# Last transformer of a four-layer kernel: scores of 128 queries in four quarters of the array, passes dealt to free slots, inverse norms by exp(-0.5 ln), a new plan of times

## The reference

```python
h = shift_token(x); q, k, v = split(h @ wqkv)        # 8 heads of 64
q, k = rotary_xpos(l2norm(q) * qs, l2norm(k) * ksc)  # l2norm: t / clip(norm(t), 1e-12)
# windows of 64 queries, each over its own and the previous 64 keys, causal within 64
attn = softmax(where(mask, -max, q @ k.T * 8)); o = attn @ v
x = x + o @ wo
h = layernorm(shift_token(x)) @ w1 + b1; a, g = split(h)   # 341 each
x = x + (a * gelu(g)) @ w2 + b2
```

## Time and profile before

| | |
|---|---|
| median of three runs | 3424.36 us |
| the profiled execution's own time | 3435.19 us |
| its span (first to last instruction) | 3433.9 us |
| mean granted TensorE clock | 0.884 of full |
| PE, DVE, ACT, POOL busy, share of the span | 83%, 70%, 56%, 47% |
| last stage, by the shift of its first pass and the end | 2491 us to 3434 us |
| table loads on ACT in the whole program | 222 of 1283 ns |

### The profile page before, as it was taken

How to read it: one execution, slowest core, us unless ns; L and a number is a source line. 1 busy time by engine, 2 the same in 40 slices (tenths; PEclk the granted TensorE clock), 3 DMA queues, 4 the chain that set the end, 5 groups by cost and what they waited for, 6 DMA issues and landing times.

```text
span 3433.9 us, 40196 instructions
## 1 busy us (share of the span) xinstructions
PE 2850.7 (83%) x14610; PEld 1219.9 (36%) x14610; DVE 2404.9 (70%) x2723; ACT 1939.1 (56%) x3566; POOL 1616.5 (47%) x989
## 2 busy tenths in 40 slices
PE   6799999966678888888876898888779898898876
PEld 3233333331223333333321532222245555555543
DVE  4888853369999999999895343877566666676562
ACT  2466662244577677677765413776545556656544
POOL 2212100224768887877876011555454445445341
PEclk6799999976788888888887998999889999999998
DMA  4132200021112221221313000111000000000000
GB/s 98 31 57 42 47 3 1 34 74 26 38 37 63 43 44 38 64 40 40 60 30 112 1 0 13 25 25 25 13 22 14 20 12 22 23 12 23 12 22 25
DMA packets 79729, 114.28 MB, mean 33 GB/s; under 512 B 16270, under 2 KB 49422, under 8 KB 78106
## 3 DMA queue, kind: packets, MB, share of 16 engines
q1 hardware_dynamic: 68268, 103.06, 12.8%
q0 software_dynamic: 11264, 8.66, 1.8%
HBM read 37.69 MB, written 17.33 MB: 16 GB/s over the span
## 4 chain that ended last, share of the span: by engine, by line
PE 43%; DVE 31%; ACT 12%; issue 8%; POOL 3%; DMA 1%; SPq 0%; DVEq 0%; POOLq 0%; ACTq 0%
DVE layer_mamba_state L1399 13%; DVE psum L1388 7%; ACT L142 3%; PE psum L830 3%; PE psum L2675 3%; PE psum L2706 2%; PE psum L2253 2%; PE psum L961 2%; PE psum L1249 2%; DVE layer_peak L771 2%; PE psum L2746 2%; ACT layer_p L2869 2%; PE psum L2689 2%; PE psum L1176 2%; PE psum L810 2%
## 5 line engine op out<-in xcount | busy, mean ns | idle before, releaser
L1441 POOL TENSOR_TENSOR layer_mamba_state<-layer_mamba_state,layer_mamba_c 128x1024 f32<-128x1024 f32 x320 | 783.0, 2482 | 287.7 <-DVE layer_mamba_state L1399 281.2
L1399 DVE TENSOR_TENSOR_SCAN layer_mamba_state<-layer_mamba_decay,psum 128x1024 f32<-128x1024 f32 x320 | 731.4, 2286 | 34.9 <-DVE psum L1388 1.0
L1249 PE MATMUL psum<-layer_mamba_state,two_to_one 128*64 128x512 f32 x1280 | 414.2, 735 | 53.8 <-DVE layer_mamba_x L1416 34.1
L771 DVE TENSOR_REDUCE layer_peak<-psum 128x2 f32<-128x1024 f32 x256 | 308.4, 1222 | 72.6 <-PE psum L742 68.0
L844 ACT ACTIVATE layer_exps<-psum 128x1024 f32<-128x1024 f32 x256 | 255.9, 1023 | 153.7 <-PE psum L810 153.7
L142 ACT ACT_TABLE_LOAD x222 | 284.8, 1283 | 66.3 <-DVE layer_scale L2969 22.9
L1328 ACT ACTIVATE layer_mamba_decay<-layer_mamba_delta_wide,layer_weights 128x511 f32<-128x511 f32 x384 | 250.4, 711 | 16.9 <-DMA layer_mamba_delta_wide<-layer_mamba_delta 8.9
L1388 DVE TENSOR_TENSOR psum<-psum,layer_mamba_u_wide 128x1024 f32<-128x1024 f32 x192 | 236.1, 1230 | 31.4 <-DMA layer_mamba_u_wide<-layer_mamba_work 20.6
L3063 POOL TENSOR_TENSOR layer_qk<-layer_qk,layer_v_between 128x1024 f32<-128x1024 f32 x64 | 150.7, 2354 | 207.3 <-DVE layer_v_between L2963 207.3
L3076 POOL TENSOR_TENSOR layer_p<-layer_p,layer_stats 128x512 f32<-128x512 f32 x128 | 132.7, 1040 | 240.0 <-DVE layer_stats L2999 239.9
L2869 ACT ACTIVATE layer_p<-psum,layer_stats 128x128 f32<-128x128 f32 x512 | 180.8, 369 | 89.3 <-DVE layer_stats L2992 86.6
(11 more groups left out here) (344 smaller groups left out, 5737.6 us busy)
## 6 DMA issues: line engine op xcount, KB each, us to landing
layer_mamba_delta_wide<-layer_mamba_delta SPq DMA_DIRECT2D x96, 128.0 KB, 2.3
layer_mamba_u_wide<-layer_mamba_work SPq DMA_DIRECT2D x96, 128.0 KB, 2.4
attn<-layer_mamba_delta SPq DMA_DIRECT2D x64, 128.0 KB, 2.4
attn<-layer_mamba_work SPq DMA_DIRECT2D x64, 128.0 KB, 2.4
layer_v_between<-layer_v SPq DMA_DIRECT2D x16, 512.0 KB, 4.3
qk_dram<-layer_qk_parts SPq DMA_DIRECT2D x16, 384.0 KB, 2.9
layer_q_rows<-qk_dram SPq DMA_DIRECT2D x96, 64.0 KB
layer_k_rows<-qk_dram SPq DMA_DIRECT2D x96, 64.0 KB
```

Source lines behind the costliest of these rows:

```text
L771: dve.tensor_reduce(self.peak[s][:, block, 2 * g:2 * g + 2], c.psum[:, at:at + 2, :], AX.X, ALU.max).then_inc(self.maxed, 1)
L1249: e = pe.matmul(c.psum[j * HALF:(j + 1) * HALF, self.sum_banks[h], :], c.two_to_one[:, :], self.state[i % len(self.state)][:, j, :], start ...
L1399: dve.tensor_tensor_scan(state, decay, self.fill.rearrange("p j t -> p (j t)"), 0.0, ALU.mult, ALU.add).then_inc(self.scanned, 1)
L1441: pool.tensor_tensor(state, state, self.both(self.c_wide[turn % self.C_BUFFERS][:, :]), ALU.mult).then_inc(self.multiplied, 1)
```

## The change

Four edits, all within `Ffn3` but for one mask.

1. Scores are taken for 128 queries, that is two windows, in one group: two mask products into two banks, then 16 score products. Head j of a pair writes bank j, window g of the block goes to array columns and PSUM partitions 64g to 64g+63, so that the four products (j, g) of a pair stand in four quarters of the array. The number of products is the same (72 for a pass). Maximum, exponentials, reciprocal, multiplication, transposes and copy are as many and as large as before, now by head j of the pair in place of window. The products with v of both windows stand in one group, which waits for both copies.
2. Passes are dealt out in the order (first four sequences, depth 0), (the same, depth 1), (last four, depth 0), (the same, depth 1), number n to slot n mod 3, a third of a period (127.5 planned us) apart: slot 0 has six passes, slots 1 and 2 have five.
3. The inverse norm is exp(-0.5 ln(max(squares, 1e-24))): a DVE maximum, then Ln and Exp on ACT, both in the table set that the exponentials use. Root and DVE reciprocal go.
4. The planned times of all steps are new.

```diff
+PLAN_F = FfnPlan(
+    make=(2.0, 9.8, 17.6, 25.4), ..., root=31.9, inverse=33.5, scale=(34.5, 32.21, 38.7, 40.38),
+    turn=(40.76, 44.24, 46.5, 48.22), ..., score=(42.38, 55.6, 68.6, 81.4), scored=(4.92, 5.52),
+    maxed=(2.0, 3.2), exp=(2.8, 5.0), sum_inverse=(5.14, 6.74), weight=(5.47, 7.7), weight_turn=(8.4, 9.96), ...
+    weight_kept=(9.2, 11.4), weigh=13.71, weighed=-0.17, keep=15.31, out=100.0, out_added=3.93,
+    ..., gelu=3.26, ..., mlp=125.8, mlp_added=3.48, gate=134.45, update=0.9, period=127.5)
+PASSES3 = [(half * SEQS // 2 + b, d) for half in range(2) for d in range(DEPTH) for b in range(SEQS // 2)]
...
-        for t, b in enumerate(range(s, SEQS, SLOTS3)):
-            for d in range(DEPTH):
-                r = t * DEPTH + d
-                yield b, d, r, (s / SLOTS3 + r) * PASS3
+        for n in range(s, len(PASSES3), SLOTS3):
+            yield *PASSES3[n], n // SLOTS3, n / SLOTS3 * PLAN_F.period
...
+    def pe_score(self, s, r, t, now):
...
+        banks = [self.banks.take(("scores", s, 2 * n + j), now, now + PLAN_F.scored[j]) for j in range(2)]
+        for at in banks:
+            c.wait_bank(at)
+            pe.matmul(c.psum[:, at, :], c.ident16[:, :], mask, start=True, stop=False)
         for i in range(PAIRS3):
-            for j in range(2):
-                rows = slice(DIM3 * j, DIM3 * (j + 1))
-                e = pe.matmul(c.psum[rows, at, i * P + gap:(i + 1) * P], q[rows, i, queries], k[rows, i, keys],
-                              start=False, stop=i == PAIRS3 - 1)
+            for j, g in ((0, 0), (1, 1), (0, 1), (1, 0)):
+                rows, window = slice(DIM3 * j, DIM3 * (j + 1)), 2 * t + g
...
+                e = pe.matmul(c.psum[g * WINDOW:(g + 1) * WINDOW, banks[j], i * P + gap:(i + 1) * P], q[rows, i, queries],
+                              k[rows, i, keys], start=False, stop=i == PAIRS3 - 1)
...
+    def pe_weigh(self, s, r, t, now):
+        own = self.banks.take(("heads_out", s, n), now, now + PLAN_F.weighed)
+        hold.wait_ge(self.p_kept[s], 2 * n + 2)
...
     def act_normalise(self, s, r):
-        self.c.table(SQRT_TABLE)
-        self.c.act.activation(scale[:, 1, :, :], scale[:, 0, :, :], ACT.Sqrt).then_inc(self.root[s], 1)
+        hold.wait_ge(self.squares_held[s], r + 1)
+        self.c.table(EXP_LN_TABLE)
+        act.activation(logs, squares, ACT.Ln).then_inc(self.root[s], 1)
...
+        act.activation(inverse, logs, ACT.Exp, scale=-0.5).then_inc(self.norms_made[s], 1)
...
     def dve_normalise(self, s, r):
-        dve.tensor_scalar(norms, norms, 1e-12, None, ALU.max).then_inc(made, 1)
-        dve.reciprocal(inverse, norms).then_inc(made, 1)
+        self.c.dve.tensor_scalar(squares, squares, 1e-24, None, ALU.max).then_inc(self.squares_held[s], 1)
```

More of the change, by code:

```diff
@@ L2323 @@
 HIDDEN_PACE3 = 1.2
[L2326 to L2335, removed]
@@ new lines @@
+PLAN_F = FfnPlan(
+    make=(2.0, 9.8, 17.6, 25.4), qkv=(0.0, 1.2, 2.4), made=(5.06, 3.5, 2.77), square=(1.2, 2.4), values=-0.1,
+    rotate=(2.28, 3.58), sums=6.53, add=4.7, root=31.9, inverse=33.5, scale=(34.5, 32.21, 38.7, 40.38),
+    turn=(40.76, 44.24, 46.5, 48.22), turned=(2.37, 2.22, 2.9), score=(42.38, 55.6, 68.6, 81.4), scored=(4.92, 5.52),
+    maxed=(2.0, 3.2), exp=(2.8, 5.0), sum_inverse=(5.14, 6.74), weight=(5.47, 7.7), weight_turn=(8.4, 9.96), weight_turned=1.07,
+    weight_kept=(9.2, 11.4), weigh=13.71, weighed=-0.17, keep=15.31, out=100.0, out_added=3.93,
+    norm=(106.4, 107.7, 109.0, 110.4, 111.3, 112.3, 111.74), glu=(116.0, 113.01, 112.87, 115.41, 116.93, 117.81),
+    glu_made=(3.46, 6.8, 5.23, 6.23), gelu=3.26, hidden=(7.1, 7.9, 8.22), mlp=125.8, mlp_added=3.48, gate=134.45, update=0.9,
+    period=127.5)
@@ L2624, in pe @@
                               self.pe_turns(s, r, start), self.pe_products(s, r, start))
-            yield start + OUT3
-            self.pe_out(s, d, r, start + OUT3)
-            yield start + NORM3[0]
+            yield start + PLAN_F.out
+            self.pe_out(s, d, r, start + PLAN_F.out)
+            first, second, logged, scaled = (start + PLAN_F.norm[n] for n in (0, 2, 3, 5))
+            yield first
             hold.wait_ge(self.shifted[s], 2 * r + 2)
-            self.banks.take(("norm", s, r), start + NORM3[0], start + NORM3[5] + 0.9)
+            self.banks.take(("norm", s, r), first, scaled + 0.9)
             self.banks.given["norm_var", s, r] = None
@@ L2633, in pe @@
             next(products)
-            yield start + NORM3[2]
-            tile.bank_b = self.banks.take(("norm_var", s, r), start + NORM3[2], start + NORM3[3] + 0.8)
+            yield second
+            tile.bank_b = self.banks.take(("norm_var", s, r), second, logged + 0.8)
             next(products)
@@ L2640, in pe_blocks @@
         for t in range(BLOCKS):
-            now = start + MAKE3[t]
+            now = start + PLAN_F.make[t]
             yield now
@@ L2672, in pe_make @@
         for which in range(2):
-            at = self.banks.take(("heads", s, n, which), now + 1.2 * which, now + 3.4 + 1.4 * which)
+            at = self.banks.take(("heads", s, n, which), now + PLAN_F.qkv[which], now + PLAN_F.made[which])
             c.wait_bank(at)
@@ L2676, in pe_make @@
             c.bank_read[at] = self.sin_made[s], 2 * n + which + 1
-        at = self.banks.take(("values", s, n), now + 2.4, now + 4.4)
+        at = self.banks.take(("values", s, n), now + PLAN_F.qkv[2], now + PLAN_F.made[2])
         c.wait_bank(at)
@@ L2685, in pe_turn_heads @@
         for which, (done, kept) in enumerate(((self.queries_turned, self.queries_kept), (self.keys_turned, self.keys_kept))):
-            at = self.banks.take(("turned", s, n, which), now + 1.0 * which, now + 1.9 + which)
+            at = self.banks.take(("turned", s, n, which), now + which, now + PLAN_F.turned[1 + which])
             c.wait_bank(at)
@@ L2714, in pe_turn @@
+    def pe_turn(self, s, r, t, j, now):
+        c, pe, p, n = self.c, self.c.pe, self.p[s][j], WINDOWS3 * r + 2 * t + j + 1
+        at = self.banks.take(("weights", s, n), now, now + PLAN_F.weight_turned)
         c.pe_hold.wait_ge(self.p_normed[s], n)
@@ L2719, in pe_turn @@
         c.bank_read[at] = self.p_kept[s], n
[L2721 to L2726, removed]
+    def pe_weigh(self, s, r, t, now):
+        c, pe, hold, p_t, n = self.c, self.c.pe, self.c.pe_hold, self.p_t[s], BLOCKS * r + t
+        own = self.banks.take(("heads_out", s, n), now, now + PLAN_F.weighed)
+        hold.wait_ge(self.p_kept[s], 2 * n + 2)
         hold.wait_ge(self.values_kept[s], BLOCKS * (r + 1))
         hold.wait_ge(self.between_ready[s], 32 * (r + 1))
[L2729 to L2736, removed]
+        c.wait_bank(own)
+        for g, v in enumerate((self.v_between[s], self.v[s])):
+            keys = slice(0 if 2 * t + g else WINDOW, P)
+            for i in range(PAIRS3):
+                first = i * P + g * WINDOW
+                for j in range(2):
+                    head = 2 * i + j
+                    e = pe.matmul(c.psum[DIM3 * j:DIM3 * (j + 1), own, first:first + WINDOW],
+                                  v[keys, t, head * DIM3:(head + 1) * DIM3], p_t[j][keys, first:first + WINDOW],
+                                  start=True, stop=True)
         e.then_inc(self.weighed[s], 1)
-        if odd:
-            c.bank_read[own] = self.heads_kept[s], BLOCKS * r + t + 1
+        c.bank_read[own] = self.heads_kept[s], n + 1
     def pe_out(self, s, d, r, now):
@@ L2761, in pe_mlp @@
         for i, rows in enumerate(GLU_ROWS):
-            now, cols, n = start + GATE3 + 1.2 * (3 + i), slice(i * P, i * P + rows), len(GLU_ROWS) * r + i + 1
+            now, cols, n = start + PLAN_F.glu[3 + i], slice(i * P, i * P + rows), len(GLU_ROWS) * r + i + 1
             yield now
-            at = self.banks.take(("glu_a", s, n), now, start + GATE3 + 7.9 + 0.8 * i)
+            at = self.banks.take(("glu_a", s, n), now, start + PLAN_F.glu[0] + PLAN_F.glu_made[1 + i])
             c.wait_bank(at)
@@ L2767, in pe_mlp @@
             c.bank_read[at] = self.hidden_made[s], n
-        now = start + MLP3
+        now = start + PLAN_F.mlp
         yield now
@@ L2972, in dve_normalise @@
     def dve_normalise(self, s, r):
-        dve, hold, made, norms, inverse = self.c.dve, self.c.dve_hold, self.norms_made[s], *(self.scale[s][:, i, :, :] for i in (1, 2))
-        hold.wait_ge(self.root[s], r + 1)
-        dve.tensor_scalar(norms, norms, 1e-12, None, ALU.max).then_inc(made, 1)
-        hold.wait_ge(made, 2 * r + 1)
-        hold.wait_ge(self.scaled[s], BLOCKS * r)
-        dve.reciprocal(inverse, norms).then_inc(made, 1)
+        squares = self.scale[s][:, 0, :, :]
+        self.c.dve_hold.wait_ge(self.summed[s], BLOCKS * (r + 1))
+        self.c.dve.tensor_scalar(squares, squares, 1e-24, None, ALU.max).then_inc(self.squares_held[s], 1)
     def dve_turn_heads(self, s, r, t):
@@ L3037, in pool_blocks @@
         for t in range(BLOCKS):
-            yield start + MAKE3[t] + 4.7
```

(10 more changed lines are left out.)

214 lines of the change are left out of this document (113 added, 101 removed).

## The result

The changed kernel takes 3251.5 us, the median of four runs (3248.9 to 3252.8), against 3429.5 (3424.0 to 3438.6): a ratio of 0.947, 95% interval 0.945 to 0.949. It is 178 us faster; the forecast was 74.5, in a range that ended at 3308. The profiled execution took 3248.9 us, its span 3247.5.

A forecast was written before the change was run, and what follows sets the result against it. PE, nearly full and paced by its clock, was taken to bound the kernel. 2491 + 124 + 12 x 50.3 + 129 + 11.8 = 3359 us of span, forecast median 3350 us, range 3308 to 3405.

The forecast's parts named there:

- Four quarters: Score products on PE: four array quarters overlap fully, so a block costs 1.59 us in place of 2.68.
- PE's work for a pass: Score products and products with v on PE: together 4.6 us less a pass.
- rival of the weight loads (e): Score groups on PE: loads wait behind the row neighbour's products, a block 4.6 us, pass 62.3, 3516 us; chance 0.02.
- rival (d): PE's clock: longer stands bring 1.2 GHz, mean clock below 0.855; at 0.80 pass 60, 3478 us; chance 0.05.
- New waits: PE's waits for banks and copies: +2.0 us a pass, with the new order alone at 0, bounds -3 to +3.
- The clock: PE in the steady passes: the clock loss of the kernel before, 2.2 us a pass, was carried over.
- Pass: Steady part of the stage: 48.1 us at full clock, 50.3 us with the clock loss.
- Opening: Start of the stage until the first pass closes: 124 us in place of 126.8.
- Last pass: End of the stage, a pass with one or no neighbour: 129 us.
- Norm: Inverse norms on ACT and DVE: exponentials come earlier, -1.0 us a pass, bounds 0 and -3.6.
- Deal: Passes at the end of the stage: evening out the slots is worth little by itself.
- Rival (c): Order of the stage: it fits so well that new waits are nil; pass 48, 3317 us; chance 0.10.

The follow-up runs named there:

- period_133: The changed kernel with only the planned period set back from 127.5 to 133.5, steps within a pass unchanged: 3467.9 us.
- chain_old: The changed kernel with only the softmax chain's planned times at the old distances, all other steps and the period new: 3509.1 us.
- t_undone: The changed kernel with all planned times of the kernel before, period 133.5, everything else as changed: 3382.4 us.
- t_alone: The changed kernel with old deal of passes, old root and reciprocal, and score products issued by diagonals; new times and two-window groups stay: 3307.2 us.
- period_130: The changed kernel with the planned period at 130.5 in place of 127.5: 3366.6 us.
- period_126: The changed kernel with the planned period at 126.0 in place of 127.5: 3350.8 us.
- d_undone: The changed kernel with the old deal of passes, slots 0 and 1 six passes and slot 2 four: 3274.4 us.
- q_alone: The changed kernel with norm, deal and planned times undone, so two-window block groups in four quarters alone: 3417.9 us.
- q_undone: The changed kernel with a block's 16 score products issued as one diagonal of all four pairs, then the other: 3282.6 us.

## Why the prediction was wrong

**Where it held.** PE bounds the stage. Four quarters work at once: 1.56 us a block against 1.59. PE's work for a pass fell by 5.3 us (47.3 to 42.0) against 4.6. The rival of the weight loads (e) is out: 32 loads go out within 0.86 us, beside the 1.10 us of their products. The Trainium skill, TensorE: Matmul & The Clock Gate, Part 3, lets loads overlap with products under way only where the row group differs; with quarters that share rows the trace disagrees once more. The rival (d) did not come about. `period_133` and `chain_old` show stands together with a lower clock (0.89 and 0.92), and are slower than the kernel before, but neither fell below its 0.855.

**The step that failed** is "New waits". It put stands and the order of the plan at +2.0 us a pass, and had the plan's own effect at 0 between -3 and +3, with "the times only set an order". PE stood 4.4 us in each full-clock pass before and 1.4 now: -3.0 in place of +2.0, 5 us a pass. The runs show that the planned times did this. Over the eleven passes of the steady stretch PE stood 5.5 us a pass before. With the old times the changed work makes it stand 7.8 (`t_undone`), 2.3 more, so the +2.0 for new waits was about right under the old order. With the new times it stands 1.4 to 1.5, whichever of the other edits is undone, and with all three undone (`t_alone`): the plan, taken at 0, was worth -6.4 us of stands a pass, beyond its bound of -3, and in all `t_undone` costs 131 us. I gave it no credit, because before, too, real passes ran longer than planned ones. But the room for a better order stood in the rows that I had read: the stands of 4.4 us, and the clock loss behind them.

**The clock** hangs on the same step. I carried 2.2 us a pass over. In the steady part of the changed kernel, with no stand above 0.7 us, the granted clock stays at 1.00 (2.4 GHz); with the old times it is 0.97 (`t_undone`), at other periods 0.97 and 0.89 (`period_130`, `period_133`). `t_alone`, with the new times but more PE work, has 1.00 too. No single length of stand decides it: the 3.57 us of the earlier trace rows lie in a stretch at 1.00, and `period_126` had 0.96 with no wait of PE above 2.8 us. What does decide it stays open.

**The sum by its terms.** Pass: 50.3 forecast, 43.4 measured. Of the 6.9 us between them 5.0 are the waits, 2.2 the clock and 0.7 more PE work saved; the 1.0 forecast for the norm goes off, since stands are counted whole here. In 12 passes this is 83 us. Opening 124 forecast, 115 measured (from 2488.2 to 2603.4), -9. Last pass 129 forecast, 111.8 measured, -17: it too had been read from passes whose order was the old one (`t_undone` has 135 here). Together 109 us; the shift of 2.8 us ahead of the stage included, this is the 112 us between 3359 and 3247.5 of span.

**Norm.** I took -1.0 us a pass. Undone alone it makes the pass 0.1 us longer and the kernel 6 us slower, no more than the batches differ; done alone it brings nothing measurable. Table loads fell from 65 to 47, as forecast (48), and this was no measure of time: the other end of the bound, 0, was right.

**Deal.** Forecast as "worth little by itself". It brings 23 us, all at the end. The prediction compared two slots with three as they were, 81% and 90% of PE busy. With the new plan three slots keep PE 97% busy, and two still only 80% (`d_undone`), so it now costs more to run two.

**Rival (c)** had the right sign and mechanism, a plan that fits, at 3317; it had 0.10, and a third of what was missing: 33 us below the forecast, where the measured time is 99 below. The undone edits add up to 31 + 6 + 23 + 131 = 191 us for 178. That the sum comes so near says little: the quarters were undone in part, the groups of two windows not at all.

## What to carry to other kernels

Where several strands share in-order engines and one engine is 90% busy, the emitted order is a resource of its own. Read its room from the stands of that engine (here 4.4 us of 51.7) plus what the clock loses (2.2), and take that, not zero, as the end that a new order may reach. Such an order fits or does not fit as a whole: one number of the plan, the period, moved by 1 to 5% cost 99 to 216 us, at the same work. So after any change of durations the order wants to be made anew. An edit tried with the old order shows little of its worth: the quarters and groups of two windows brought 20 us with the old times (`q_alone`), while under the new times undoing only part of the quarters costs 31 (`q_undone`).

## What the runs showed of the hardware

Products in four quarters of the array, two by the same rows and two by the same columns, fp32, 128 columns each, run at once: 32 records in 1.10 us. They need not be neighbours in PE's list: with the second diagonal 16 records behind the first, its products started ahead of six records that stood before them, and the group took 1.59 us, 0.3 less than two at a time would need by the earlier trace rows. And PE's granted clock was 1.00 for 564 us in which it never stood above 0.7 us, and 0.97 in `period_130`, where it stood 3.2 us in nearly every pass of 51 us; a stretch of 155 us of the kernel before kept 1.00 with a stand of 3.57 us in it.
